# Gathered rows of the first expert stage: twelve places and ten tiles ahead in place of four places and seven tiles

## The reference

```python
topk_probs, topk_idx = jax.lax.top_k(probs, 2)
gates = jnp.zeros((T, 8)).at[jnp.arange(T)[:, None], topk_idx].add(topk_probs)
for e in range(8):
    h = jax.nn.gelu(flat_x @ w1[e] + b1[e], approximate=False)   # 192 -> 288
    y = h @ w2[e] + b2[e]                                        # 288 -> 192
    out = out + y * gates[:, e:e + 1]
```

## Time and profile before

| | us |
|---|---|
| median of 3 timed runs | 460.32 (459.7 to 461.4) |
| profiled execution | 458.92 |
| its span, first to last instruction | 457.1 |
| TensorE busy in the span | 415.3 (91%) |
| VectorE, ScalarE, GpSimd busy | 292.0, 196.8, 225.8 |
| mean granted TensorE clock | 0.957 |

### The profile page before, as it was taken

How to read it: one execution, slowest core, us unless ns; L and a number is a source line. 1 busy time by engine, 2 the same in 40 slices (tenths; PEclk the granted TensorE clock), 3 DMA queues, 4 the chain that set the end, 5 groups by cost and what they waited for, 6 DMA issues and landing times.

```text
span 457.1 us, 10302 instructions
## 1 busy us (share of the span) xinstructions
PE 415.3 (91%) x3599; PEld 329.0 (72%) x3608; DVE 292.0 (64%) x1360; ACT 196.8 (43%) x374; POOL 225.8 (49%) x266
## 2 busy tenths in 40 slices
PE   8999998989768989988888979968999999999993
PEld 5653655637336878877746759824999999999993
DVE  6689999999873434344549336997466556555651
ACT  1387845541551111111025302645566656566650
POOL 5203797897055666666510000344355575665534
PEclk9899799999989988999979999997999999999997
DMA  8609300010311212212179998097233233333322
GB/s 233 98 25 238 82 1 2 1 35 1 123 52 59 67 62 69 71 60 68 61 213 231 229 228 203 7 139 149 47 54 63 42 64 63 54 57 58 52 27 28
DMA packets 40130, 39.04 MB, mean 85 GB/s; under 512 B 7576, under 2 KB 37260, under 8 KB 40080
## 3 DMA queue, kind: packets, MB, share of 16 engines
q1 hardware_dynamic: 28861, 23.05, 22.8%
q0 software_dynamic: 9312, 14.03, 15.3%
q10 hardware_dynamic: 1906, 1.30, 1.0%
HBM read 28.00 MB, written 11.06 MB: 85 GB/s over the span
## 4 chain that ended last, share of the span: by engine, by line
PE 47%; DMA 24%; DVE 9%; issue 7%; POOL 5%; ACT 5%; another core or an unknown queue 1%; POOLq 1%; ACTq 0%; SPq 0%; DVEq 0%
DMA out<-a,idx 20%; PE bank L1940 6%; PE bank L1982 6%; PE bank L2035 4%; PE bank L1802 4%; POOL reg L706 3%; PE bank L1954 2%; PE bank L1963 2%; ACT xn L833 2%; PE bank L2230 2%; DMA a<-expert_rows 2%; PE bank L1917 2%; POOL reg L737 1%; PE bank L1989 1%; PE bank L2265 1%
## 5 line engine op out<-in xcount | busy, mean ns | idle before, releaser
L737 POOL DMA_INDIRECT reg<-xn_rows,idxs x62 | 60.9, 982 | 30.3 <-issue 17.2
L1954 PE MATMUL bank<-reg,xT 64*128 64x128 f32 x1116 | 75.1, 275 | 0.7 <-DVE reg L1546 0.5
L757 POOL DMA_INDIRECT out<-a,idx x31 | 50.1, 1615 | 46.5 <-DMA out<-a,idx 35.7
L1954 PEld LDWEIGHTS bank<-reg,xT 64*128 64x128 f32 x1116 | 70.9, 188 | 1.0 <-DVE reg L1546 0.7
L1989 PE MATMUL bank<-reg 64*128 64x192 f32 x744 | 71.2, 323 | 0.0
L1989 PEld LDWEIGHTS bank<-reg 64*128 64x128 f32 x744 | 65.6, 187 | 0.0
L1802 PE MATMUL bank<-con 128*128 128x512 bf16 x184 | 50.2, 431 | 1.5 <-issue 1.3
L1044 ACT ACTIVATE reg<-reg 128x1152 f32 x31 | 36.1, 1164 | 29.3 <-PE bank L1989 29.3
L1573 DVE TENSOR_SCALAR a<-bank,gs 128x192 f32<-128x192 f32 x31 | 13.0, 418 | 53.0 <-PE bank L1989 53.0
L1023 ACT ACTIVATE reg<-bank 128x288 f32<-128x288 f32 x31 | 12.4, 410 | 77.7 <-PE bank L1940 40.6
L745 POOL DMA_INDIRECT expert_rows<-a,idx x31 | 30.6, 986 | 25.4 <-DVE a L1570 19.1
(11 more groups left out here) (363 smaller groups left out, 805.8 us busy)
## 6 DMA issues: line engine op xcount, KB each, us to landing
reg<-in_w2b SPq DMA_DIRECT2D x8, 576.0 KB, 10.0
reg<-in_w1b SPq DMA_DIRECT2D x8, 288.0 KB, 9.7
reg<-in_w1a SPq DMA_DIRECT2D x8, 216.0 KB
reg<-in_w2a SPq DMA_DIRECT2D x8, 216.0 KB
xn_rows<-xn SPq DMA_DIRECT2D x4, 384.0 KB, 2.7
reg<-in_w1b SPq DMA_DIRECT2D x8, 192.0 KB, 7.9
xn_rows<-xn SPq DMA_DIRECT2D x1, 1152.0 KB, 7.8
out<-h SPq DMA_DIRECT2D x1, 1152.0 KB
```

The source lines that it names most:

```text
L737: pool.indirect_dma_start(xs[:, i % RING, 0:(D, D2)[l]], None, xd[l], bass.IndirectOffsetOnAxis(ap=idxs[:, i:i + 1], axis=0)).then_inc(xs_ ...
L757: pool.indirect_dma_start(out, bass.IndirectOffsetOnAxis(ap=idx2[:, i:i + 1], axis=0), ys[:, i % YRING, :], None, compute_op=ALU.add).then ...
L1954: ins = MM(bank[2 + 2 * p + a][:, c * P:(c + 1) * P], w1r[rs, p, col:col + hc], xT64[rs, p, k, :], start=(c == 0 and k == 0), stop=(c == n ...
```

## The change

In the first expert stage the rows go to the twelve places of `xn` (tile i to place i % 12) in place of the four of `xs`. Each place has its own semaphore: eight new ones, and the four of the token gathers of the kernel's beginning, which start from 32 (`XS0_BASE`). The first five gathers wait for nothing; gathers 5 to 11 wait for `tx_mm` >= i - 3, as before; gathers 12 to 30 wait for `tx_mm` >= i - 11, the transposition of tile i - 12. `ahead` is 10. The second expert stage keeps its waits and its order.

```diff
+RING0 = NJ
+BURST = 5
+        xs0_ready = [sem(f"xs0_ready{s}") for s in range(RING0 - 4)] + gath
+        XS0_BASE = [0] * (RING0 - 4) + [16 * B // 4] * 4
                 def gather(i):
+                    if l == 0:
+                        if i >= BURST:
+                            pool.wait_ge(tx_mm, i - (3 if i < RING0 else RING0 - 1))
+                        pool.indirect_dma_start(xn[:, i % RING0, :], None, xd[0],
+                                                bass.IndirectOffsetOnAxis(ap=idxs[:, i:i + 1], axis=0)
+                                                ).then_inc(xs0_ready[i % RING0], 16)
+                        return
                     if i >= RING:
-                        pool.wait_ge(tx_ev if l else tx_mm, l * NT + i - RING + 1)
-                    pool.indirect_dma_start(xs[:, i % RING, 0:(D, D2)[l]], None, xd[l],
+                        pool.wait_ge(tx_ev, NT + i - RING + 1)
+                    pool.indirect_dma_start(xs[:, i % RING, :], None, xd[1],
-                ahead = RING + (3, 2)[l]
+                ahead = (RING0 - 2, RING + 2)[l]
                 def t_x(i):
-                    s = i % RING
-                    pe.wait_ge(xs_ready[s], 16 * (turns(l, i, RING) + 1))
                     if l == 0:
+                        pe.wait_ge(xs0_ready[i % RING0], XS0_BASE[i % RING0] + 16 * (i // RING0 + 1))
                         for k in range(NK):
-                            ins = nc.tensor.transpose(bank[s % 2][0:KC, k * P:(k + 1) * P],
-                                                      xs[:, s, k * KC:(k + 1) * KC], ident)
+                            ins = nc.tensor.transpose(bank[i % 2][0:KC, k * P:(k + 1) * P],
+                                                      xn[:, i % RING0, k * KC:(k + 1) * KC], ident)
```

More of the change, by code:

```diff
@@ L1911, in t_x @@
                 def t_x(i):
-                    s = i % RING
-                    pe.wait_ge(xs_ready[s], 16 * (turns(l, i, RING) + 1))
                     if l == 0:
+                        pe.wait_ge(xs0_ready[i % RING0], XS0_BASE[i % RING0] + 16 * (i // RING0 + 1))
                         for k in range(NK):
-                            ins = nc.tensor.transpose(bank[s % 2][0:KC, k * P:(k + 1) * P],
-                                                      xs[:, s, k * KC:(k + 1) * KC], ident)
-                    else:
+                            ins = nc.tensor.transpose(bank[i % 2][0:KC, k * P:(k + 1) * P],
+                                                      xn[:, i % RING0, k * KC:(k + 1) * KC], ident)
+                    else:
+                        s = i % RING
+                        pe.wait_ge(xs_ready[s], 16 * (turns(0, i, RING) + 1))
                         if i >= 2:
```

## The result

The changed kernel took 464.23 us (median of ten runs) against 460.01 us of the kernel before in the same comparison: a ratio of 1.0099, interval 1.0071 to 1.0128. It is slower by 1%, 4.2 us. The forecast was 460.2 us in a range of 456.8 to 463.8.

The account below looks back on a forecast made before the run. TensorE was taken as the bound in the first stage's quiet stretch (2.50 us per loop), GpSimd nearly as long. Terms 0 - 0 - 0.1 + 0 + 0 = -0.1 us gave 460.2 us, range 456.8 to 463.8.

Parts of the forecast that it names:

- I price the new destination at 0: First-stage gathers into the twelve places: same gathers, bytes, queue and transposes, array already free; cost 0.
- the sum: Whole kernel: 0 - 0 - 0.1 + 0 + 0 = -0.1 us, giving 460.2 us on the median.
- Ten ahead: GpSimd's first-stage queue: gathers 8 to 10 precede scatter 0, starting it 3.0 us later, near 149.9; cost 0.
- the queues meet again at scatter 7: First-stage scatters: delayed from scatter 0, they regain the old timing at scatter 7, which started at 168.42 before.
- cost 0: Later scatters 0 to 6: only VectorE's output copies could wait, with 16 us of cover; 3.0 us without it.
- The fifth gather: First stage: the fifth gather loses its wait; none of these waits was felt, so removing one saves 0.
- the longer lead: First-stage gathers issued earlier: 0.1 us expected saving from avoiding late landings, with 0 and 2.4 us as ends.
- the waits stay at 0.9 and 0.5 us: TensorE's waits for gathered rows at tiles 1 and 4 lie in an unchanged burst, so 1.4 us stay.
- late increments grow: First stage, 148 to 168 us: busier GpSimd delays increments, bringing another clock drop; 463.7 to 465.6 us, chance 0.15.
- TensorE was waiting for rows: First stage: VectorE's waits hide tiles standing for gathers; later pauses and half clock go, 8.2 us, 452.1; chance 0.06.
- A clock drop goes away: Half-clock stretch at 168.7: a shorter pause before it brings back 3.40 us, 456.9 us; chance 0.13.
- The lead isn't what it says: First stage: ten tiles of lead exist only from gather 12 on; changes nothing, counted within the forecast's 0.66.

Follow-up runs that it names:

- x2: Kernel before, with only the first stage's gathers moved to the changed kernel's twelve semaphores, still four places and seven tiles ahead; ratio 1.0116.
- x9: Changed kernel, ten tiles ahead, with the second stage's gathers going on with the same twelve semaphores; ratio to the kernel before 1.0024.
- x11: Changed kernel with the second stage's gathers going on with the same twelve semaphores, and seven tiles ahead; ratio to the kernel before 1.0020.
- x4: Changed kernel with its twelve places and semaphores, but seven tiles ahead as in the kernel before; ratio to the kernel before 1.0108.
- x19: Changed kernel with first-stage gathers 12 to 30 issued into unused places, TensorE not waiting for them (computation partly left out); one run, 464.72 us.
- x15: Changed kernel with first-stage gathers 12 to 30 left out, the tiles reusing rows already in place (computation partly left out); one run, 453.50 us.
- x22: Kernel before with three more GpSimd drains: one after the table's 8 gathers, two in a row between the stages; one run, 465.13 us.
- x12: Changed kernel, ten tiles ahead, with one more GpSimd drain between the two expert stages; ratio to the kernel before 1.0073.
- x5: Kernel before, with the first stage's gathers on the four semaphores of the token gathers, none new; one run, 466.5 us.
- x7: Kernel before, with the first stage's gathers on eight semaphores: the second stage's four and four new ones; one run, 468.3 us.

## Why the prediction was wrong

**The step that failed** is "I price the new destination at 0", and the sum that was built on it. Of the new places I priced the array and left out the semaphores that came with them, and the sum ended with the stage at 228 us; it had no row of what closes the kernel, though GpSimd's closing row stands at the end of the profile's chain of work (452.07 us, line 100), with the whole kernel's transfers behind it. x2 shows the term: 12 semaphores alone, +4.3 us of closing drain, ratio 1.0116. x9 and x11 show it from the other side: the same places and either order with the semaphores used again, 5.7 us of drain and 1.002. Why such semaphores lengthen the drain stays open. None of the four rivals had this in it.

**Ten ahead.** Scatter 0 was put near 149.9 and came at 150.41, gather 10 near 148.7 and came at 149.16. That no one would wait for these scatters was right: no copy of VectorE waited for a place. That the queues meet again at scatter 7 was wrong: it started at 170.61, not at 168.42. In the profile the stage became 1.8 us longer and the end 0.7 us later, so "cost 0" was off by that much; x4's stage of 94.3 us speaks for the order as the cause, GpSimd's missing pause as the reason is argued only.

**The fifth gather and the longer lead.** The fifth gather's wait was worth nothing, as said. TensorE waited for rows twice, 0.34 and 0.40 us, at tiles 0 and 1; tile 4's wait is gone. That the waits stay at 0.9 and 0.5 us was off by 0.7 us in all. With the same beginning they were 0.47 and 0.34 us in x19, but 1.55, 0.79 and 0.64 us (tiles 0, 1 and 3) in x15, so the 0.7 us is no gain of the change: these waits differ from one execution to the next by more than that. From tile 5 on nothing waits for rows, as before. Earlier issue paid nothing that can be seen; here the rows spoke rightly against the rule of the Trainium skill, "DMA: Bandwidth & Descriptors", section "Rules for kernel authors", to issue early and wait late: the first stage's transfers were overlapped already.

**The rival "late increments grow"** was right that transfers under way cost TensorE pauses here (x15, x19), but that the measured 464.2 us lies in its span of 463.7 to 465.6 is chance: most of the loss is the drain. VectorE's long wait moved on to output tile 4, whose copy came 2.4 us later (159.10 for 156.69), where I had up to 1.86; TensorE pauses and the clock drops earlier, and a further drop follows at about 200 us. But the price of 3.4 us or more took a whole new drop of 6.8 us without anything given back; the first drop replaced the old one, and the stage lost 1.8 us in all. My argument against it, that GpSimd's pause might be only the consequence of late copies, is not settled: x15 and x19 show what the transfers do, but no run takes away the pause alone.

**The rival "TensorE was waiting for rows"** is refuted by x19: from tile 12 on TensorE waits for no rows, and the pauses stay. The 12 us that x15 gained belong to the transfers. **"A clock drop goes away"** did not happen in the changed kernel: the drop moved from 168.7 to 162.1. **"The lead isn't what it says"** was so, and without effect.

## What to carry to other kernels

A sum that ends with the stage that a change touches leaves out what the kernel settles at its end: look at each engine's last instruction, and at how long it outlasts the last useful one. Where GpSimd issues many transfers, try letting later transfers use the semaphores of earlier ones, and compare the closing drain when they change: here that was worth 3.5 us of drain (9.2 to 5.7), for a reason that stays open. When an engine pauses without waiting for data, leave the transfers of another queue out for once, as x15 does: the 10 us that the kernel before loses to them are far more than the 2.4 us that the prediction set as the most a longer lead could win.

## What the runs showed of the hardware

A GpSimd drain took 5.12 us with 62 transfers behind it and 5.79 with 70 (x22, x12), although all had landed: 0.083 us each, if it goes by transfers. With none it took 0.05 us (x22). The closing drain took 4.8 us in the kernel before and 9.1, 8.1 and 8.7 us in x2, x5 and x7, which differ from it only by the semaphores of the first stage's gathers.

Gathers between the scatters on GpSimd cost the first stage time even where TensorE didn't wait for their rows. Without gathers 12 to 30 it took 83.6 us in place of 95.9, and between 163 and 206 us TensorE was busy for 43.00 of 43.00 us at full clock in place of 37.92 at 0.89. With these gathers, but no wait of TensorE for their rows (x19), it was 96.5 us and 37.58 at 0.90, with pauses of 1.3 to 1.8 us.
